# A preLN decoder layer on one core: the cross attention's output projection is scheduled three blocks of keys later, and the last pair's sums of weights go to VectorE

## What is computed

```python
q = (query @ Wq + bq).reshape(b, sq, 16, 64)
k = (key @ Wk + bk).reshape(b, key.shape[1], 16, 64)
v = (value @ Wv + bv).reshape(b, value.shape[1], 16, 64)
scores = jnp.einsum('bqhd,bkhd->bhqk', q, k) / 8
attn = jax.nn.softmax(scores, axis=-1)
out = jnp.einsum('bhqk,bkhd->bqhd', attn, v).reshape(b, sq, 1024)
out = out @ Wo + bo + residual
...  # layer norm of out, added to x; then x + product(layernorm(x))
```

## Time and profile before

| | |
|---|---|
| median of 3 runs | 2157.15 us |
| lowest and highest | 2141.80, 2167.85 us |
| the profiled execution, its own time | 2139.68 us |
| its span on the core | 2137.7 us |
| mean granted PE clock in it | 0.911 of full speed |
| busy: PE, PEld, DVE, ACT, POOL | 1862.8, 949.8, 1295.8, 916.6, 1036.1 us |

### The profile page before, as it was taken

One profiled execution on the slowest core, in us unless ns is written; L12 is line 12 of the kernel. 1 busy time (PEld: TensorE's weight loads), 2 busy tenths in 40 slices (PEclk: granted clock), 3 DMA queues, 4 the chain that ended last, 5 costly groups with the idle time before them and its releaser, 6 DMA issues.

```text
span 2137.7 us, 29456 instructions
## 1 busy us (share of the span) xinstructions
PE 1862.8 (87%) x10650; PEld 949.8 (44%) x10650; DVE 1295.8 (61%) x2455; ACT 916.6 (43%) x1866; POOL 1036.1 (48%) x872
## 2 busy tenths in 40 slices
PE   6888999889998998898999899889889889989671
PEld 3544444434444544444445445445445445444331
DVE  4677766766712557746636545645654653667888
ACT  2235655555644343244343343344344434434331
POOL 1000000000000466558777777877876886886664
PEclk9669999998967899999999899999999999999875
DMA  5222201240011000000000000000000000000001
GB/s 106 29 33 32 32 8 25 32 88 1 1 30 40 19 1 1 1 10 12 1 1 12 1 1 12 1 1 12 2 1 3 1 1 3 1 10 21 0 21 39
DMA packets 28745, 34.46 MB, mean 16 GB/s; under 512 B 4099, under 2 KB 26948, under 8 KB 26948
## 3 DMA queue, kind: packets, MB, share of 16 engines
q1 hardware_dynamic: 28600, 32.59, 8.5%
HBM read 14.99 MB, written 4.19 MB: 9 GB/s over the span
## 4 chain that ended last, share of the span: by engine, by line
PE 47%; issue 26%; POOL 10%; DVE 8%; ACT 6%; SPq 2%; DMA 1%; POOLq 0%; ACTq 0%; DVEq 0%
PE psum L924 8%; POOL parts_room L698 7%; PE psum L809 7%; PE psum L904 6%; PE psum L784 5%; PE psum L757 4%; PE psum L947 4%; ACT weights_room L1007 3%; PE psum L889 3%; DVE maxima L1189 3%; PE psum L723 2%; POOL parts_room L1434 2%; PE psum L821 2%; ACT weights_room L1079 1%; PE psum L793 1%
## 5 line engine op out<-in xcount | busy, mean ns | idle before, releaser
L1189 DVE TENSOR_REDUCE maxima<-psum 128x1 f32<-128x400 f32 (+5 forms) x1664 | 864.1, 579 | 351.5 <-PE psum L889 192.4
L698 POOL TENSOR_TENSOR parts_room<-parts_room,weights_room 128x512 f32<-128x512 f32 (+1 forms) x606 | 761.2, 1284 | 133.1 <-ACT weights_room L1079 128.1
L1079 ACT ACTIVATE weights_room<-psum 128x512 f32<-128x512 f32 (+1 forms) x757 | 402.2, 601 | 568.8 <-PE psum L904 387.3
L1007 ACT ACTIVATE weights_room<-psum 128x512 f32<-128x512 f32 (+3 forms) x640 | 297.8, 535 | 248.2 <-PE psum L784 133.8
L1396 POOL TENSOR_SCALAR rstd<-meanvar 128x2 f32<-128x2 f32 (+1 forms) x24 | 8.0, 333 | 708.6 <-DVE meanvar L1139 708.6
L904 PE MATMUL psum<-stack_room,dk_hi 64*128 64x512 f32 (+1 forms) x1408 | 269.4, 410 | 18.7 <-ACT weights_room L1079 18.7
L889 PE MATMUL psum<-k_later,stack_room 64*128 64x400 f32 (+1 forms) x896 | 245.5, 404 | 33.1 <-DVE maxima L1189 32.0
L784 PE MATMUL psum<-stack_room,stack_room 51*128 51x512 f32 (+3 forms) x640 | 201.6, 452 | 45.9 <-ACT weights_room L1007 44.5
L889 PEld LDWEIGHTS psum<-k_later,stack_room 64*128 64x128 f32 x896 | 129.5, 184 | 205.3 <-issue 103.2
L924 PE MATMUL psum<-weights_room,parts_room 128*64 128x512 f32 (+1 forms) x754 | 211.5, 627 | 0.0
L924 PE MATMUL psum<-weights_room,late_room 128*64 128x512 f32 (+1 forms) x760 | 208.9, 622 | 0.0
(11 more groups left out here) (133 smaller groups left out, 1987.5 us busy)
## 6 DMA issues: line engine op xcount, KB each, us to landing
stack_room<-parts_room SPq DMA_DIRECT2D x96, 128.0 KB
x_block<-x_dram SPq DMA_DIRECT2D x8, 512.0 KB, 4.8
x_middle<-x_block SPq DMA_DIRECT2D x4, 512.0 KB, 3.1
x_block<-x_middle SPq DMA_DIRECT2D x4, 512.0 KB, 3.9
out_dram<-x_block SPq DMA_DIRECT2D x8, 256.0 KB, 2.1
parts_room<-ctx_dram SPq DMA_DIRECT2D x1, 1536.0 KB
stack_room<-shift_rows SPq DMA_DIRECT2D x64, 2.0 KB
parts_room<-wq_dram SPq DMA_DIRECT2D x8, 128.0 KB, 2.2
```

What stands on the lines that cost most here:

```text
L698: engine.tensor_tensor(sum_[:kw, :], old[:kw, :], weights[u % NP_WEIGHTS][:kw, :], ALU.add) \
L1007: engine.activation(w_self[s % NW][:, m, 0:n], self_scores[(HP * s + m) % SELF_SCORES][:, 0:n], ACT.Exp, scale=SELF_SCALE).then_inc(exp_do ...
L1079: engine.activation(weights[u % NP_WEIGHTS][:kw, :], pair_scores[u % NSCORES][:kw, :], ACT.Exp, scale=CROSS_SCALE).then_inc(pair_exp, 1)
L1189: engine.tensor_reduce(maxima[:, p % 2, i // TB, n, i % TB, ch:ch + 1], bank_of(use + n)[:, 0:real - k0], AX.X, ALU.max) \
```

## The change

Two things. PROJECT_LAG becomes TB + 7 = 11 steps for pairs 0 to 6, and the last pair has a lag of its own, TB + 3 = 7. And in the last pair both heads' adds are VectorE's, where they stand at the stage `pair_values` of their step and not at `pair_scores`; POOL has none there. `added_with`, which tells the count of the semaphore that an add raises, now looks it up in a table made from the steps in their order.

```diff
--- before.py
+++ after.py
@@ -26,7 +26,7 @@
 FOLD_LAG, TURN_LAG, OUT_LAG = 2, 2, 2
 
 
-SUMS_LAG, PROJECT_LAG = 4, TB + 4
+SUMS_LAG, PROJECT_LAG, LAST_PROJECT_LAG = 4, TB + 7, TB + 3
 
 SELF_RING, SELF_SCORES = 4, 3
 CROSS_RING, NSCORES = 3, 4
@@ -226,7 +226,7 @@
         for t in range(TB):
             self.after(t + 1, lambda t=t: self.put("pair_invert", p, b, t))
         self.after(TB + 1, lambda: self.put("pair_divide", p, b))
-        self.after(PROJECT_LAG, lambda: self.pair_out(p, b))
+        self.after(PROJECT_LAG if p < NP - 1 else LAST_PROJECT_LAG, lambda: self.pair_out(p, b))
 
     def pair_sweep2(self, p):
         batch = []
@@ -474,17 +474,9 @@
 
         return HP * (pair_step_of[p, b, NS - 1] + 1)
 
-    def on_vector(p, m):
-
-        return p == NP - 1 and m == HP - 1
-
-    def added_with(p, b, j, m):
-
-        done = (NS - 1) * pair_finish_no[p, b] + max(1, j)
-        if on_vector(p, m):
-            return added_on_vector, done - (NS - 1) * NB * (NP - 1)
-        alone = (NS - 1) * max(0, pair_finish_no[p, b] - NB * (NP - 1)) + (max(1, j) if p == NP - 1 else 0)
-        return added_on_pool, HP * (done - alone) + alone - (HP - 1 - m if p < NP - 1 else 0)
+    def on_vector(p):
+
+        return p == NP - 1
 
 
     consts_set = sem("consts_set")
@@ -517,6 +509,17 @@
     y_scaled, y_biased, y_added = sem("y_scaled"), sem("y_biased"), sem("y_added")
     inverse_made, w8_scaled, w8_made = sem("inverse_made"), sem("w8_scaled"), sem("w8_made")
     dve_step, pool_step = sem("dve_step"), sem("pool_step")
+
+
+    added_made, made = {}, {True: 0, False: 0}
+    for p, b, j, _ in pair_scores_at:
+        for m in range(HP if j else 0):
+            made[on_vector(p)] += 1
+            added_made[p, b, j, m] = added_on_vector if on_vector(p) else added_on_pool, made[on_vector(p)]
+
+    def added_with(p, b, j, m):
+
+        return added_made[p, b, max(1, j), m]
 
     CROSS_USE = next(s.use for s in stages if s.kind == "cross_start")
 
@@ -1271,10 +1274,10 @@
                         src = bank_of(use)[:kw, (ta - t0) * P:(tb - t0) * P].rearrange("p (t d) -> p t d", d=P)
                         last = engine.tensor_tensor(v_pair[p % 2][:kw, ta:tb, :], src, bias, ALU.add)
                 last.then_inc(emptied(use), 1)
-            elif kind == "pair_scores":
+            elif kind == "pair_values":
                 p, b, j, s = at
                 for m in range(HP):
-                    if j and on_vector(p, m):
+                    if j and on_vector(p):
                         add(dve, engine, p, b, j, s, m)
             elif kind == "pair_invert":
                 p, b, t = at
@@ -1425,7 +1428,7 @@
             elif kind == "pair_scores":
                 p, b, j, s = at
                 for m in range(HP):
-                    if j and not on_vector(p, m):
+                    if j and not on_vector(p):
                         add(pool, engine, p, b, j, s, m)
             elif kind == "pair_divide":
                 n_block = pair_finish_no[at]
```

## The result

| | before | changed |
|---|---|---|
| median of four runs each, same chip | 2149.48 us | 2014.96 us |
| lowest to highest | 2138.02 to 2167.85 | 2014.69 to 2051.62 |
| ratio of the times, 95% interval | | 0.9366 [0.9275, 0.9458] |

The kernel is 6.3% faster; 2035 was forecast. It is also the one that was profiled with this result, and it lost its extra time in self attention, which the change doesn't touch; so rows of after come from a second profile of the same kernel (experiment 9, 2008.84 us), except where the first is named.

A forecast was written before the change was run, and what follows sets the result against it. PE's work, waits and low-clock stretches were taken to bound the kernel. -94 - 13 + 5 - 3 = -105 against the profiled 2139.7 us gave 2035, own range 2010 to 2060.

The forecast's parts named there:

- The bound of the steady pairs: PE's time sets the end: its work, its waits (72.9 us for GpSimd's divide) and its stretches at 1.2 GHz.
- The pair's sum: A later pair's block intervals become 31.9, 36.6, 31.5 and 50.1 us; over 979.75 to 1924.79 this gives -94.
- The bank cost: The projection at its new place may wait for PSUM banks: 0.2 us each taken, +5 us, between 0 and 22.
- Part 2: Last pair, both heads' adds on VectorE beside the values: 149.2 us against 151.9 from its first projection on, -3.
- The tail's relief: Last pair: the tail's other instructions with two SBUF inputs no longer meet POOL's adds, a gain without a price.
- 1, the clock does not come back: Rival for the pairs' stalls: the waits go but the clock stays low; 2069 us, chance 9%.
- 2, POOL becomes the bound: Rival for intervals b = 0 and 2: POOL's 30.9 us, lengthened, sets them; 2055 to 2079 us, chance 7%.
- 3, POOL's wide instructions hold VectorE's additions: Rival in the last pair: seven wide POOL instructions a late block delay adds, some 18 us; 2053 us, chance 10%.
- 4, additions stay at 1.58: Rival in the last pair: VectorE's adds take 1.58 us each whatever POOL does; 2115 us, chance 3%.
- 5, long stretches at the low clock for PE's running without pause: Rival in pairs 0 to 6: PE running without pause loses the clock for long; 400 us gives 2190, chance 2%.
- 6, the wait only moves: Rival in pairs 0 to 6: POOL's lag grows until PE waits at the sums instead; 2137 us, chance 3%.
- The median: Whole kernel: 2035 us predicted as the median too, 5.7% less, as the spread was put down to clock behind stalls.

The follow-up runs named there:

- experiment 9: The changed kernel itself, timed and profiled again with nothing altered: 2016.71 us against 2142.12 for the kernel before, ratio 0.9403.
- experiment 1: The kernel before with only the projection's lag raised from 8 to 11 in pairs 0 to 6: 2028.90 us against 2141.23, ratio 0.9488.
- experiment 10: The changed kernel with the last pair's projection lag at 8 instead of 7: 2020.83 us against 2142.12 for the kernel before, ratio 0.9402.

## Why the prediction was right, point by point

**The bound of the steady pairs: right.** PE's time with its waits and its clock set B. Waits 71.9 and clock 34.4 us were measured for the whole of B. The forecast had 62.9 + 10 and 31 + 3 over all projections, 106.9 together, ahead of the +5 for banks; experiment 1's B and its 2.2 us of C give 108.5.

**The pair's sum: right, its parts not as shown.** 31.9 + 36.6 + 31.5 + 50.1 = 150.1 us was the forecast, 148.9 is the sum of the four intervals. The sign to look for, b = 0 and 2 near 31.7, was badly put: a projection that moves into the next block takes the cut along, and the intervals are 37.8, 42.7, 32.2 and 36.2. For the same reason "POOL idle under 1 us" was wrong. POOL's busy time of a pair, 127.2 us in those four rows, is what it was, and its idle is 1.5 us in the shortest interval and 9.8 in the longest.

**The bank cost: too high.** +5 us was taken, between 0 and 22. The row shows 2.9 us in 6 waits of at most 0.5, for ScalarE's release of a bank, not VectorE's.

**Part 2: right in its sign and mis-sized, -3 forecast.** From the last pair's first projection to the end, VectorE's windows before and after:

```profile
1983.73:2137.70 153.97, 131.01 (x234) 0.74 0.06 21
```
```profile
1868.10:2007.00 138.90, 130.22 (x264) 0.77 0.07 23
```

and the additions alone (DVE, then POOL):

```profile
1983.73:2137.70 153.97, 29.64 (x26) 34.59 (x25) 0.74 0.06 21
```
```profile
1868.10:2007.00 138.90, 44.76 (x56) 0.00 (x0) 0.77 0.07 23
```

That is 15.1 us shorter. Term by term: *idle*, forecast 22.9 down to 9.5, measured 153.97 - 131.01 = 23.0 down to 138.90 - 130.22 = 8.7, and no addition waits for an exponential any more: right. *Additions*: 56 x 0.80 = 44.8 us, where 0.71 had been taken, 5 us more. In blocks 0 and 1 they did take what was forecast, 0.69 us (24.31 us for 35, from 1832 to 1868). *The tail's relief*, which the forecast named and left without a price: the two lines above fell from 16.9 + 15.4 to 9.6 + 8.5, 14.2 us. This is the term whose absence makes the error. How the adds and the tail share what is left hangs on what meets what: in experiment 10 the adds took 0.69 us each (38.4 us for 56) and the relief was 6.0. Against the forecast's price for 56 adds, 39.8 us, the two together are 9.2 us better in the changed kernel and 7.4 in experiment 10. It could have been priced, roughly, from the trace of before: 32 instructions that ran at some 1.0 us, beside additions which stretch from 0.68 to 1.58. The other lines changed by less than 2 us together. The rest of C's 19.6 us lies before the first projection, 44.2 us before and 39.7 now, 2.2 of the difference the stall that part 1 took away, the other 2.3 not separated. Blocks 0 and 1 stayed under PE, as costed. The 28 us ahead of the last pair's first projection, all five engines:

```profile
1840.24:1868.10 27.86, 27.86 (x159) 12.30 (x155) 23.79 (x35) 15.26 (x30) 3.23 (x2) 1.00 0.00 1
```

PE is busy in all of it, VectorE in 23.8 us.

**The rivals.** *1, the clock does not come back*: refuted, 0.99 and 1.00 in B. *2, POOL becomes the bound*: refuted, no wait of PE for POOL in B. *3, POOL's wide instructions hold VectorE's additions*: true in kind, small in size. The mean of 0.80 over 0.71 is 5 us, not 18, nothing of it is seen in the adds of experiment 10, and it was outweighed by the relief. The Trainium skill, "SBUF — State Buffer", section "Who interferes with whom", has the rule that a VectorE instruction with two SBUF inputs and a GpSimd instruction that reads SBUF shut each other out. The traces agree: the tail's instructions took 1054 and 963 ns with POOL adding, 600 and 533 in the changed kernel, and 911 and 732 in experiment 10, where POOL's tail work met them. *4, additions stay at 1.58*: refuted. *5, long stretches at the low clock for PE's running without pause*: not in B (its 2190 should read 2195, 2035 + 400 x 0.4). *6, the wait only moves*: refuted, no wait at the sums in B.

**The median.** The sum was made against the profiled execution, 2139.7, and the spread between runs put down to the stalls in the pairs. That step was wrong: with the stalls gone the changed kernel still spreads over 37 us, and the two profiles put it in A, 778.4 against 732.2 us at 0.81 and 0.89. The sum keeps A at its 740.3 us, and that the median run had much the same is luck: between the two profiles A alone moved by 46 us. The forecast was 20 us above the median. Without A, B and C lie 17.6 and 21.0 us under the forecast -105 in the two profiles. Part 2 explains 14.4 of it (196.0 to 178.6 where 3 was forecast), the bank cost 2, and the rest is in the pairs' sums.

## What to carry to other kernels

Follow a stall to what its releaser is queued behind: here either end of the wait could be moved, and moving the divide one step earlier gave the same B as moving the projection three steps later. Price a PE stall with its echo in the clock, here 34 us on 72, and separate the two with filler matmuls that fit the wait. When work is moved off an engine, look for every instruction of the others that ran slower beside it, and not only for those that are moved; and judge by all such lines together, since what one is spared another may meet.

## What the runs showed of the hardware

- Work of no use, put where PE waits for 1.6 to 3.8 us, made the kernel faster: B had the clock at 1.00 instead of 0.96 and was 34.4 us shorter, although 27 fillers of 3.70 or 1.98 us stood in it, 77.5 us in all.
- Not every stall is followed by the low clock. Behind two waits of 1.58 us, at 1220.85 and 1555.68, the eight matmuls of the projection took 3.78 and 1.99 us, with the clock at 0.50 from 1220.85 to 1226 and at 1.00 from 1553 to 1560. What decides it no run here shows.
- An f32 multiplication of 128x128 by 128x512 is two instructions on PE: 7 calls gave x14 in 6.28 us, 0.45 us from one to the next.
- The low clock in self attention differs from one execution to the next for the same program (0.81 to 0.89 over A), and by the two profiles that is where this kernel's spread comes from. What sets it off is open; no experiment here was made on it.
